# Attention: the maxima's score item ahead of the exponentials' score item on TensorE

## The reference

```
proj = layer_norm(x) @ W_in.T + b_in
q, k, v, p, y = split(proj)
k = (1 - smear) * k + smear * k_prev
pos = cumsum(sigmoid(y))
mask = causal - (pos_i - pos_j)
scores = (q / s) @ (k / s).T / sqrt(16) + mask
o = softmax(scores) @ v
out = layer_norm((silu(p) * o) @ W_out.T)
```

## Time and profile before

| | |
|---|---|
| median of 3 runs | 2007.17 us (2002.69 to 2007.68) |
| profiled execution | 1999.75 us |
| its span | 1997.7 us |
| PE busy | 1679.8 us (84%) |
| PEld busy | 1273.2 us (64%) |
| DVE busy | 1188.4 us (59%) |
| ACT busy | 758.6 us (38%) |
| POOL busy | 352.3 us (18%) |

### The profile page before, as it was taken

The page is one execution under the profiler, slowest core; times in us unless marked ns, Lnnn a source line. Parts: engine busy times, 40 slices in busy tenths (PEclk is TensorE's granted clock), DMA queues, the critical chain, the costliest instruction groups (busy, mean ns, idle before and its releaser), DMA issues. The chain is left out here.

```text
span 1997.7 us, 64778 instructions
## 1 busy us (share of the span) xinstructions
PE 1679.8 (84%) x24643; PEld 1273.2 (64%) x24643; DVE 1188.4 (59%) x5605; ACT 758.6 (38%) x2596; POOL 352.3 (18%) x547
## 2 busy tenths in 40 slices
PE   3877777899999999999999988458989789897757
PEld 2367676788888888888888866224545345544423
DVE  4655555666666666666666644446676566675365
ACT  2522222222233323232323222114665466575645
POOL 4000000000000000000000012462223314311144
PEclk9955555555555555555555555567999899998878
DMA  5000000000000000000000000076435624741001
GB/s 117 0 18 16 18 16 18 19 17 16 16 16 16 15 16 16 16 16 16 16 16 16 16 5 0 2 122 95 65 53 83 99 28 75 100 64 19 1 6 37
DMA packets 99297, 65.54 MB, mean 33 GB/s; under 512 B 30830, under 2 KB 98950, under 8 KB 99206
## 3 DMA queue, kind: packets, MB, share of 16 engines
q1 hardware_dynamic: 95094, 63.79, 18.6%
q10 hardware_dynamic: 4112, 0.55, 0.2%
HBM read 31.77 MB, written 15.47 MB: 24 GB/s over the span
## 5 line engine op out<-in xcount | busy, mean ns | idle before, releaser
L672 PE MATMUL PS<-G,W 128*128 128x8 f16 x18432 | 579.8, 169 | 92.3 <-DVE G L845 88.0
L672 PEld LDWEIGHTS PS<-G,W 128*128 128x128 f16 x18432 | 545.6, 105 | 170.5 <-DVE G L845 145.0
L1588 DVE TENSOR_REDUCE MX<-PS 128x1 f32<-128x512 f32 (+3 forms) x352 | 223.0, 636 | 194.4 <-PE PS L1335 192.7
L776 ACT ACTIVATE tr<-PS 128x16 f32<-128x16 f32 x512 | 94.7, 185 | 549.6 <-PE PS L672 549.6
L1491 ACT ACTIVATE PT<-PS 128x512 f32<-128x512 f32 (+1 forms) x352 | 193.9, 559 | 176.2 <-PE PS L1351 172.5
L831 DVE SCALAR_TENSOR_TENSOR u_<-tr,PS 128x16 f32<-128x16 f32 x512 | 87.4, 171 | 257.2 <-PE PS L672 248.0
L678 PE MATMUL PS<-XS,ident 128*128 128x64 f32 x516 | 171.8, 436 | 6.0 <-DMA XS<-XI 5.9
L778 ACT ACTIVATE tz<-PS 128x16 f32<-128x16 f32 x512 | 94.2, 184 | 192.0 <-PE PS L672 192.0
L1332 PE MATMUL PS<-KS,QS 99*128 99x256 bf16 (+3 forms) x512 | 136.2, 318 | 32.5 <-DMA KS<-k_parts 20.8
L643 POOL TENSOR_TENSOR rt<-mv,eps 128x1 f32<-128x1 f32 x96 | 18.4, 191 | 705.9 <-DVE mv L866 705.9
L1348 PE MATMUL PS<-QS,KS 102*128 102x256 bf16 (+3 forms) x512 | 132.6, 311 | 4.5 <-issue 3.0
(11 more groups left out here) (281 smaller groups left out, 2725.1 us busy)
## 6 DMA issues: line engine op xcount, KB each, us to landing
XS<-XI SPq DMA_DIRECT2D x130, 96.0 KB, 1.9
QS<-q_parts SPq DMA_DIRECT2D x48, 256.0 KB
KS<-k_parts SPq DMA_DIRECT2D x48, 256.0 KB
q_parts<-PQ SPq DMA_DIRECT2D x16, 384.0 KB, 13.0
k_parts<-PK SPq DMA_DIRECT2D x16, 384.0 KB, 13.5
HS<-HR SPq DMA_DIRECT2D x128, 32.0 KB, 1.7
X<-in_L_attn_x_dram SPq DMA_DIRECT2D x8, 256.0 KB, 7.7
out_dram<-X SPq DMA_DIRECT2D x8, 256.0 KB, 2.3
```

Of the source, the lines that this page charges most:

```text
L672: return pe.matmul(bank[:, p, o:o + B], W[:, kc, w:w + P], G[:, kc, :], start=False, stop=True, skip_group_check=True)
L776: act.activation(tr[:, :], pR[:, p, o:o + NSTEP], ACT.Tanh, scale=gate_scale).then_inc(hn_tr.sem, 1)
L1588: dve.tensor_reduce(MX[:, g % 2, heads[0]:heads[-1] + 1, NT - 1 - it], p_x[:, k % 2, 0:len(heads) * w].rearrange("p (a w) -> p a w", w=w), ...
```

## The change

In `item` on PE, the maxima's item is now called ahead of the exponentials' item. The wait for the maxima's rows stays ahead of both. The other engines' orders are not touched.

```diff
@@ -1383,9 +1383,9 @@
                     if j == 0:
 
                         pe.wait_ge(m_in.sem, m_in.value(pe, b, 4 * g + n + 1))
-                    exp_item(b, p, g, j, n)
                     if ahead:
                         maxima(*ahead, j, n)
+                    exp_item(b, p, g, j, n)
                     if j >= 1 and n == len(ITEMS[j]) - 1:
                         if j == 1:
                             if g == 0:
```

## The result

The kernel became faster: 1992.16 us median of 6 runs (1987.58 to 1994.31) against 2005.12 us of the kernel before beside it, a ratio of 0.9934 with a 95% interval of 0.9915 to 0.9953. I had forecast 2009.4 us. A second comparison gave 0.9943 [0.9922, 0.9963], 1993.36 against 2003.57 us. One of the six runs of the kernel before took 3915.55 us; without it their median is 2003.07 us. The profiled execution took 1987.9 us, 1985.8 of them its span (before 1997.7). I measure the attention stage from the start of its first exponential to the end of its last: 518.6 us before, 507.2 after. So 11.4 of the 11.9 us of span lie in it.

What follows compares the result with a forecast made beforehand. PE was taken as nearest to full (60.1 of 67.8 us in sequence 4), with DVE and ACT close enough to hold it up. 1.2 us in sequences 1 to 5 plus 1.0 at the DMA wait gave +2.2: 2009.4 us, range 2000 to 2018.

Steps and rivals of the forecast that it cites:

- Steps 1 and 2: Group 0: maxima's transposes that wait for XN shift by -0.45 us, the product that waits for XT by -0.17.
- Step 3: Group 0 into group 1: DVE's CAST ends with POOL's product, PE's gain is waited away; transposes behind KA at +0.06 us.
- step 4: Group 1, item 8: exponentials' item +0.64 us at half clock, +0.33 at full; transposes behind KAT at +0.70 or +0.39.
- step 5: Group 1, item 10: exponentials' item 0.45 us later, then ACT's copy GT; PE's products behind it at +1.15 or +0.84.
- step 6: Group 2, item 3: maxima's item 0.28 us earlier, DVE then full up to ON; shift +0.87 or +0.56.
- step 7: Group 2, item 10: maxima's item 0.45 us earlier, DVE full up to ON of group 3; shift +0.42 or +0.11.
- e8: Exponentials' item with k = 8; in group 1 behind maxima's item m8, +0.64 us at half clock, +0.33 at full.
- rival C: Longer waits in group 1 bring one more half-clock stretch per sequence: +12 us, 2019 us; chance 0.09.
- DMA term: Sequence 6, PE's wait for sequence 7's stacks: chain starts 0.45 us later, up to 0.64 more follows; +1.0 us taken.
- A: Waits for ON are what counts, each of 30 shrinks by 0.23 to 0.28 us: -6.7 us, 2000.5 us; chance 0.15.
- B: Costs at group 1's items 8 and 10 paid, later gains not returned: +6 to +7, 2013.7 us; chance 0.12.
- D: Every shift is covered, no effect: 2007.2 us; counted with the main forecast, chance 0.64 together.

Runs made afterwards that it cites:

- warm_before: Order of before with extra products on PE in its waits of groups 0 and 1, against the kernel before: 0.9956 [0.9942, 0.9971].
- warm_after: Changed order with extra products on PE in its waits of groups 0 and 1, against the kernel before: 0.9901 [0.9875, 0.9926].
- only_810: Maxima's item first only at items 8 and 10 of group 1, against the kernel before: 1.0031 [1.0012, 1.005], 2009.59 us.
- only_seq0: Maxima's item first in sequence 0 only, against the kernel before: 0.9982 [0.9968, 0.9995], -3.6 us.
- pool_hold0: Order of before, POOL's first split of k in sequence 0 held until DVE finished its steps for k, against the kernel before: 0.9982 [0.9972, 0.9993], -3.6 us.
- not_seq0: Maxima's item first in sequences 1 to 7 only, against the kernel before: 0.9966 [0.9953, 0.9979], -6.8 us.
- only_k36: Maxima's item first only at items 3 to 6 of every group, against the kernel before: 1.0007 [0.9987, 1.0027], 2002.48 us.
- after_again: Changed kernel, unchanged, timed in five more rounds against the kernel before: 0.9943 [0.9922, 0.9963], 1993.36 against 2003.57 us.
- e_first_act: Maxima's item first everywhere but at items 8 and 10 of group 1, against the kernel before: 0.9938 [0.9916, 0.9961], 1992.05 us.
- best: Order of e_first_act with extra products in PE's waits in sequences 1 to 5, against the kernel before: 0.9914 [0.9899, 0.9929], 1983.33 us.

## Why the prediction was wrong

The direction and the size were wrong: +2.2 us forecast, -11 to -13 us measured. The time lies below the range's lower end of 2000. By its own steps:

- **Steps 1 and 2 held.** `XN` is waited for 0.44 us less, `XT` 0.27 us more.
- **Step 3 had the right mechanism and the wrong size.** POOL's product and DVE's CAST still end together, at 1650.98 and 1651.05 us:

```profile
1648.48 2.50 POOL L1240 TENSOR_TENSOR ON<-ON,SP 128x1024 f32<-128x1024 f32 x1 [0.26 <-POOL PQ L1221]
```

```profile
1649.50 1.55 DVE L1601 CAST QA<-MX 128x16 bf16<-128x16 f32 x1
```

  I measure from the first product of the pair in item 0 of sequence 4, 1638.07 before and now

```profile
1629.88 0.39 PE L1332 MATMUL PS<-KS,QS 99*128 99x512 bf16 x1
```

  Against it POOL's product ended at 21.34 us before and ends at 21.10 after: 0.24 us earlier, where I had +0.06. `QF` comes 0.06 later as I said, but the product takes 2.50 instead of 2.69 us and POOL's work ahead of it is 0.1 us shorter. My step took POOL's lengths as fixed. So the gain of group 0 is not waited away.
- **Steps 4 to 7 held, each taken by itself.** At the full clock, measured in the same way in `warm_before` and `warm_after`:

| point, in sequence 4 | forecast | measured | its own step: forecast, measured |
|---|---|---|---|
| transposes that wait for `KA` (step 3) | +0.06 | -0.21 | |
| transposes behind `KAT` (step 4) | +0.39 | +0.13 | +0.33, +0.34 |
| products behind `GT` (step 5) | +0.84 | +0.54 | +0.45, +0.41 |
| maxima's transposes, group 2 (step 6) | +0.56 | +0.26 | -0.28, -0.28 |
| maxima's transposes, group 3 (step 7) | +0.11 | -0.19 | -0.45, -0.45 |

  The whole difference at the end, 0.30 us, is the error of step 3; over five sequences it is 1.5 us. `only_810` shows steps 4 and 5 alone.
- **"Sequence 0 has no output work and I count it as nothing" failed.** In the traces it is the largest single miss: both pairs show -5.4 and -5.3 us in it, and `only_seq0` gives -3.6 us in time. With no output work, no `GT` and no gate product, the steps that cost (4 and 5) are worth only 0.33 us there (`only_810`), and those that gain remain. The prediction took a sequence to be 66 to 70 us long, while this one had 62.0. I should have seen that the sum over the round does not hold where half of its terms are missing, and followed this sequence in the timeline as I did the fourth. There a shift of a few tenths also turned the meeting of DVE and POOL (1.1 us, `pool_hold0`), and 2 to 3 us at half clock went.
- **The clock was taken only as a price at e8.** I chose between two values for m8's length and gave rival C, more half clock, a chance of 0.09. The opposite, that a shorter wait spares a stretch at half clock, I did not put a price on. In group 0 it is what counts: 5 of 12 groups before had one at some 1.2 us each, 0 of 12 after. In four groups that makes 2.0 us, of the 2.9 that sequences 1 to 5 lost in these traces. The earlier trace rows had shown two values of the clock for equal sequences, 0.95 and 0.97: it does not come from the work alone, and may go either way.
- **The DMA term failed in size**: +1.0 forecast for it and 0 for the rest of the sequence, -0.2 to -0.5 measured over groups 0 to 2 of sequence 6. Its second part is there: the next product stands 1.15 us behind PE's restart instead of 0.64, +0.5 us. The queue's own time to the restart varies between 33.3 and 33.9 us in the four traces, as much as the term, and group 0 is 0.31 us shorter (11.39 to 11.08). What else outweighed it differs between the two pairs and stays open.
- **By time, more is missed outside sequence 0.** `not_seq0` gives -6.8 us where my sum had +2.2. The traces show -2.9 in sequences 1 to 5 and -0.6 to -0.8 in 6 and 7, so some 3 us of it are in no trace; the interval of the -6.8 is 4 to 9 us.

Of the rivals, A had the sign and a good half of the size, but not the reason: the waits for `ON` did shrink, by 6.1 us in all, but `only_k36`, where they shrink as much, is no faster. B is what `only_810` measures, its gains left out. C and D fell.

**What stays open.** The number of stretches at half clock changes from one execution of a kernel to another, so how much of the median's gain is clock I know only from six traces, and these are not typical runs: the one of before (1999.75 us) is faster than all six timed beside after, that of `after_again` (1998.35) the slowest of its six. Open too are the 3 us of sequences 1 to 7 that no trace shows, why POOL's work became shorter in step 3, the last 1.0 us of sequence 0's group 1, the pause that `warm_after` doesn't have, and why `e_first_act` isn't faster than after.

## What to carry to other kernels

Where two items change places, read for each stage which copy stands behind each of them on the other engines, and do the sum again where the stage's work differs (the first sequence, the last): a sum for the steady round says nothing of them. Where a busy PE waits one or two us in each round and its clock falls behind such a wait, a shift of tenths can spare or add a stretch at half clock that is worth more than the shift; products put into the wait took 2.3 us off a group of 19 and made the two fastest kernels here, `warm_after` (0.9901) and `best` (0.9914). A cost on a chain of copies, as at items 8 and 10, is found by doing that piece alone.

## What the runs showed of the hardware that I had not expected

- DVE against POOL: the same DVE instruction takes 0.47 or 1.39 us (line 1554) and 0.74 or 1.66 us (line 1557), by whether it starts 0.14 and 0.20 us ahead of POOL's or 0.08 and 0.03 us behind.
- Some 16 added products in a group of 19 us made it 2.3 us shorter; the clock stayed at 1.00 instead of 0.82.
- A pause of 5.3 to 9.3 us at the hardware loop's edge, on PE in twelve traces and on DVE in one, is absent in one of the 14.
